# Carrying weight and result place in each row of a routed expert layer, and scattering the results instead of fetching them by index

## The reference

```
logits = xf @ Wg                                  # xf: layernormed tokens, N x 128
topw, topi = top_k(logits, 2); topw = softmax(topw)
comb[n, topi[n]] += topw[n]
gu = einsum('nd,edh->enh', xf, Wgu) + bgu         # 8 experts, 2 x 256 hidden
g, u = split(gu); h = silu(g) * u
eo = einsum('enh,ehd->end', h, Wd) + bd
out = h_in + einsum('end,ne->nd', eo, comb)       # weighted sum of the two experts
```

## Time and profile before

| | |
|---|---|
| median of 3 runs | 820.52 us (817.84 to 821.28) |
| the profiled execution's own time | 824.18 us |
| its span, first to last instruction | 822.4 us |
| busy: PE, DVE, ACT, POOL | 603.9, 430.1, 264.7, 498.1 us |
| mean granted TensorE clock | 0.835 of full |
| indirect DMAs on POOL | 180 to `xbuf`, 180 from `ybuf` |
| chain that ended last | PE 37%, POOL 21%, DVE 14%, issue 13%, DMA 7% |

### The profile page before, as it was taken

The page is one execution under the profiler, slowest core; times in us unless marked ns, Lnnn a source line. Parts: engine busy times, 40 slices in busy tenths (PEclk is TensorE's granted clock), DMA queues, the critical chain, the costliest instruction groups (busy, mean ns, idle before and its releaser), DMA issues.

```text
span 822.4 us, 12791 instructions
## 1 busy us (share of the span) xinstructions
PE 603.9 (73%) x3335; PEld 519.1 (63%) x3335; DVE 430.1 (52%) x1708; ACT 264.7 (32%) x690; POOL 498.1 (61%) x520
## 2 busy tenths in 40 slices
PE   3787645327778788698989986999898969999000
PEld 2687634316567576586878875888787758888000
DVE  4789655343556657265655766355544623445122
ACT  2502122112234432244442543254253324444000
POOL 5602327763655756377677776477777767760674
PEclk9998855557789988698997997899999979999555
DMA  7185000126345533565655663667577768984221
GB/s 152 53 290 148 1 0 26 33 90 186 101 127 153 145 104 106 164 194 150 185 169 154 205 198 106 191 202 218 179 214 235 236 197 257 279 279 147 80 77 61
DMA packets 84597, 125.23 MB, mean 152 GB/s; under 512 B 15044, under 2 KB 57792, under 8 KB 84526
## 3 DMA queue, kind: packets, MB, share of 16 engines
q1 hardware_dynamic: 72526, 101.66, 40.9%
q0 software_dynamic: 11520, 22.35, 9.5%
q10 hardware_dynamic: 480, 0.41, 0.4%
HBM read 84.25 MB, written 43.25 MB: 155 GB/s over the span
## 4 chain that ended last, share of the span: by engine, by line
PE 37%; POOL 21%; DVE 14%; issue 13%; DMA 7%; ACT 3%; SPq 3%; POOLq 0%; DVEq 0%; ACTq 0%
PE gu L587 15%; PE dn L587 11%; POOL gat L1048 8%; POOL xbuf L1034 8%; PE mx L587 5%; POOL rs L966 3%; DMA gat<-ybuf,ypos 3%; PE xTp L765 3%; DMA space<-xbuf 2%; DMA space<-in_x_dram 2%; PE tr L587 2%; ACT x L894 1%; PE tr L719 1%; DVE gat L1485 1%; DVE rec L1268 1%
## 5 line engine op out<-in xcount | busy, mean ns | idle before, releaser
L1034 POOL DMA_INDIRECT xbuf<-x,pos x180 | 186.4, 1035 | 112.9 <-DVE pos L1369 56.0
L587 PE MATMUL gu<-space,wts 128*128 128x256 f32 x912 | 246.0, 410 | 9.1 <-DVE space L1476 9.1
L1476 DVE SCALAR_TENSOR_TENSOR space<-gu,wts,space 128x256 f32<-128x256 f32 x228 | 109.1, 482 | 235.7 <-ACT space L912 173.3
L1048 POOL DMA_INDIRECT gat<-ybuf,ypos x180 | 177.7, 987 | 87.9 <-issue 55.5
L912 ACT ACTIVATE space<-gu,wts 128x256 f32<-128x256 f32 x228 | 109.1, 479 | 305.7 <-PE gu L587 305.3
L587 PEld LDWEIGHTS gu<-space,wts 128*128 128x128 f32 x912 | 174.8, 206 | 32.0 <-DVE space L1476 10.9
L587 PEld LDWEIGHTS dn<-wts,space 128*128 128x128 f32 x912 | 127.9, 204 | 14.1 <-DVE space L1476 7.1
L587 PE MATMUL dn<-wts,space 128*128 128x128 f32 x912 | 129.1, 288 | 5.8 <-DVE space L1476 5.8
L765 PE MATMUL xTp<-cst,space 128*128 128x128 f32 x228 | 51.8, 311 | 40.2 <-DMA space<-xbuf 38.1
L765 PEld LDWEIGHTS xTp<-cst,space 128*128 128x128 f32 x228 | 26.7, 154 | 52.6 <-DMA space<-xbuf 40.8
L966 POOL TENSOR_TENSOR rs<-ve,nhalf 128x4 f32<-128x4 f32 (+2 forms) x39 | 40.4, 1036 | 29.7 <-DVE ve L1281 15.2
(11 more groups left out here) (198 smaller groups left out, 837.8 us busy)
## 6 DMA issues: line engine op xcount, KB each, us to landing
wts<-wall SPq DMA_DIRECT2D x114, 386.0 KB
space<-xbuf SPq DMA_DIRECT2D x114, 128.0 KB, 2.6
ybuf<-space SPq DMA_DIRECT2D x114, 128.0 KB
xbuf<-zero_rows SPq DMA_DIRECT2D x4, 1024.0 KB, 10.5
xt<-in_txt_dram SPq DMA_DIRECT2D x16, 256.0 KB, 3.0
xbuf<-zero_rows SPq DMA_DIRECT2D x32, 128.0 KB
out_dram<-gat SPq DMA_DIRECT2D x16, 256.0 KB
xbuf<-x,pos POOLq DMA_INDIRECT x180
```

Of the source, the lines that this page charges most:

```text
L587: return nc.tensor.matmul(o, l, r, start=a, stop=z_)
L1034: nc.gpsimd.indirect_dma_start(out=xbuf, out_offset=bass.IndirectOffsetOnAxis(pos[0:p, c:c + 1], 0), in_=x2[n % NX2][0:p, m // 2 * D:(m // ...
L1048: nc.gpsimd.indirect_dma_start(out=gat[b][0:p, (k * W4 + j) * D:(k * W4 + j + 1) * D], out_offset=None, in_=ybuf[g], in_offset=bass.Indire ...
L1476: V.scalar_tensor_tensor(hid[q % 4], gu_ps[q % 3][:, SLOT:2 * SLOT], wts[k % NW][:, W_B + HT + t:W_B + HT + t + 1], sil[q % 3], ALU.add, A ...
```

## The change

Rows of `xbuf` become 130 numbers wide: 128 of data, the token's weight for this expert, and the integer place in a new buffer `results` at which the result row belongs. `x2` holds each row twice (one for each expert), the second a copy by ACT. `weights` writes weight and place into them. `row_keep` multiplies the result by the weight that came with the row (two operations in place of one copy), and POOL scatters each tile's 256 result rows with two indirect DMAs to `results` (`scatter_rows`, 228 in all), where a chunk's rows lie in the order of its tokens. SP loads them plainly, one DMA a chunk (`load_results`), and `combine` is two additions. `ybuf`, `store_tile`, `gather`, `places_of_results` and `w2` are gone. Padding rows have places of their own: POOL numbers the zero rows once for the spare regions, waits until these have been written, and numbers them again for `pad`. `text_y` moves from POOL to DVE. The row tile is now held until its results are scattered (`load_tile` waits for tile k-7; 7 buffers in place of 5).

```
@@ slots, buffers
-ITERS = 30
+ITERS = 33
-          z_T=(3, 11), text_decay=(3, 12), text_sums=(3, 13), text_y=(2, 0),
+          z_T=(3, 11), text_decay=(3, 12), text_sums=(3, 13), text_y=(3, 14),
+          ... x_copy=(2, 15),
-NX = 5
+NX = 7
-NG = 4
+NG = 3
+LOADS_AT = by_slot([p for g, (a, b) in enumerate(GROUPS) for p in spread(list(range(a, b)), LOAD_FROM[g], LOAD_TO[g])])
+ROW = D + 2
-    xbuf = nc.dram_tensor("xbuf", (ROW0[-1], D), F32, kind="Internal").ap()
+    xbuf = nc.dram_tensor("xbuf", (ROW0[-1], ROW), F32, kind="Internal").ap()
+    results = nc.dram_tensor("results", (RESULT_ROWS, D), F32, kind="Internal").ap()
@@ SP
-            sp.wait_ge(W.zero_ok, 1)
+            sp.wait_ge(W.spare_ok, 1)
             for g in range(len(GROUPS)):
...
             def load_tile(k):
...
-                wait(sp, W.xTt_ok, k - NX + 1)
+                if k >= NX:
+                    sp.wait_ge(yrow_out[(k - NX) % NYB], stored_before(k - NX))
...
-            def store_tile(k):
...
+            def load_results(n):
+                b, g, p = n % NG, group_of(n), parts(n)
+                if n == GROUPS[g][0]:
+                    for m in range(TILE0[g + 1] - NYB, TILE0[g + 1]):
+                        sp.wait_ge(yrow_out[m % NYB], stored_before(m))
+                wait(sp, W.sum_ok, n - NG + 1)
+                r0 = n * A_CHUNK
+                sp.dma_start(res[b][0:p, 0:2 * width(n) * D].rearrange("p (j c) -> p j c", j=width(n)),
+                             results[r0:r0 + p * 2 * W4, :].rearrange("(p j k) d -> p j (k d)", p=p, k=2)[:, 0:width(n)]
+                             ).then_inc(res_in[b], 16)
@@ ACT
+            def x_copy(n):
+                p, w = parts(n), width(n)
+                act.wait_ge(W.x2_ok, n + 1)
+                rows = x2[n % NX2][0:p, :].rearrange("p (k j c) -> p k j c", k=2, j=W4)
+                copy(rows[:, 1, 0:w, 0:D], rows[:, 0, 0:w, 0:D]).then_inc(W.copy_ok, 1)
@@ row_keep
-                copy(yrow[k % NYB], dn_ps[k % 2][:, 0:SUB * D]).then_inc(W.y_row_ok, 1)
+                for s in range(SUB):
+                    last = nc.scalar.activation(yrow[k % NYB][:, s * D:(s + 1) * D], dn_ps[k % 2][:, s * D:(s + 1) * D], ACT.Copy,
+                                                scale=xrow[k % NX][:, s * ROW + D:s * ROW + D + 1])
+                last.then_inc(W.y_row_ok, 1)
@@ POOL
-            def text_y(n):
...
             def scatter(n, m):
...
-                    pool.wait_ge(W.x2_ok, n + 1)
+                    pool.wait_ge(W.meta_ok, n + 1)
+                    pool.wait_ge(W.w1_ok, n + 1)
+                if m == 1:
+                    pool.wait_ge(W.copy_ok, n + 1)
...
-            def gather(n, j, k):
...
+            def scatter_rows(k):
+                pool.wait_ge(W.y_row_ok, k + 1)
+                for s in range(SUB):
+                    place = xrow[k % NX][:, s * ROW + D + 1:s * ROW + D + 2].bitcast(I32)
+                    nc.gpsimd.indirect_dma_start(out=results, out_offset=bass.IndirectOffsetOnAxis(place, 0),
+                                                 in_=yrow[k % NYB][:, s * D:(s + 1) * D], in_offset=None
+                                                 ).then_inc(yrow_out[k % NYB], 16)
+            def number_pads(base):
+                ids = zero_rows[:, :].bitcast(I32).rearrange("p (e s c) -> p e s c", e=E, s=SUB)[:, :, :, D + 1]
+                return nc.gpsimd.iota(ids, [[SLOT, E], [1, SUB]], base=base, channel_multiplier=SUB)
+            pool.wait_ge(W.zero_ok, 1)
+            pool.wait_ge(W.seen_zero, 2)
+            number_pads(SPARE_ROW).then_inc(W.spare_ok, 1)
+            pool.wait_ge(W.spare, 16 * len(GROUPS))
+            number_pads(PAD_ROW).then_inc(W.pads_ok, 1)
...
-                    for n, j, k in gathers(i, s):
-                        gather(n, j, k)
+                    for k, t in units(i, s):
+                        if t == 1:
+                            if k >= 2 and not any(first_of_group(m) for m in range(k - 1, k + 1)):
+                                scatter_rows(k - 2)
+                            if last_of_group(k):
+                                scatter_rows(k - 1)
+                                scatter_rows(k)
@@ DVE
             def weights(n):
...
-                w0, w1 = [w2[0:p, (n * 2 + k) * W4:(n * 2 + k) * W4 + w] for k in range(2)]
+                meta = x2[n % NX2][0:p, :].rearrange("p (k j c) -> p k j c", k=2, j=W4)
+                wait(dve, W.w1_ok, n)
+                w0, w1 = [meta[:, k, 0:w, D] for k in range(2)]
+                dve.wait_ge(W.x2_ok, n + 1)
+                V.tensor_scalar(meta[:, :, 0:w, D + 1].bitcast(I32), place0[0:p, :].rearrange("p (k j) -> p k j", k=2)[:, :, 0:w],
+                                n * A_CHUNK, None, ALU.add).then_inc(W.meta_ok, 1)
...
-            def places_of_results(g):
...
             def combine(n):
...
+                V.tensor_tensor(rows[:, :, 0], rows[:, :, 0], rows[:, :, 1], ALU.add).then_inc(W.half_ok, 1)
                 dve.wait_ge(W.half_ok, n + 1)
...
+                V.tensor_tensor(h, h, rows[:, :, 0], ALU.add).then_inc(W.sum_ok, 1)
```

More of the change, by code:

```diff
@@ L183, in opens, with loads @@
     return OPENS_AT.get(i * SLOTS + s, [])
-def gathers(i, s):
-    return GATHERS_AT.get(i * SLOTS + s, [])
+def loads(i, s):
+    return LOADS_AT.get(i * SLOTS + s, [])
 def combines(i, s):
@@ L279, in program @@
         top[0] = 6 * ROWS
-        xrow = [part(SUB * D) for _ in range(NX)]
+        xrow = [part(SUB * ROW) for _ in range(NX)]
         xT = [part(SLOT) for _ in range(2)]
@@ L287, in program @@
         h_txt = [part(W4 * D) for _ in range(B)]
[L289 to L292, removed]
+        res_all = sb("res", [P, NG * 2 * W4 * D])
+        res = [res_all[:, i * 2 * W4 * D:(i + 1) * 2 * W4 * D] for i in range(NG)]
+        rows2_raw = res_all[0:2, 0:W4 * D + E * D]
+        rows2_hi = res_all[0:2, W4 * D + E * D:2 * (W4 * D + E * D)].bitcast(F32R)
         wts = [sb(f"wts{i}", [P, W_COLS]) for i in range(NW)]
@@ L303, in program @@
         yT = sb("yT", [P, W4 * D])
-        x2 = [sb(f"x2{i}", [P, W4 * D]) for i in range(NX2)]
+        x2 = [sb(f"x2{i}", [P, 2 * W4 * ROW]) for i in range(NX2)]
         x2T = sb("x2T", [P, W4 * D])
@@ L387, in program @@
         yrow_out = [sem(f"s_yrow_out{i}") for i in range(NYB)]
-        gat_in = [sem(f"s_gat_in{i}") for i in range(NG)]
-        gat_out = [sem(f"s_gat_out{i}") for i in range(NG)]
+        res_in = [sem(f"s_res_in{i}") for i in range(NG)]
         sent = [sem(f"s_sent{i}") for i in range(NX2)]
@@ L425, in stored_before, with loaded_before @@
         def stored_before(k):
-            return 16 * (k // NYB + 1)
-        def gathered_before(n):
-            return 16 * sum(2 * width(m) for m in range(n % NG, n + 1, NG))
-        def out_before(n):
-            return 16 * sum(width(m) if m < IMG_CHUNKS else 1 for m in range(n % NG, n + 1, NG))
+            return 16 * SUB * (k // NYB + 1)
+        def loaded_before(n):
+            return 16 * (n // NG + 1)
         @block.sync
@@ L564, in _ @@
                                 load_tile(k + AHEAD)
-                        else:
-                            if k >= 2 and not any(first_of_group(m) for m in range(k - 1, k + 1)):
-                                store_tile(k - 2)
-                            if last_of_group(k):
-                                store_tile(k - 1)
-                                store_tile(k)
                     if due("text_load", i, s):
@@ L577, in _ @@
                         store_out(n)
+                    for n in loads(i, s):
+                        load_results(n)
                     for g in opens(i, s):
@@ L580, in _ @@
                             load_tile(TILE0[g] + k)
-            for m in range(CHUNKS - NG, CHUNKS):
-                sp.wait_ge(gat_out[m % NG], out_before(m))
+            sp.wait_ge(W.out, 16 * sum(1 if n >= IMG_CHUNKS else width(n) for n in range(CHUNKS)))
         @block.tensor
@@ L764, in tile_T @@
                 for s in range(SUB):
[L765 removed]
+                    last = nc.tensor.transpose(xT_ps[:, s * P:(s + 1) * P], xrow[k % NX][:, s * ROW:s * ROW + D], ident)
                 last.then_inc(W.xTt_ok, 1)
@@ L1502, in _ @@
                             tile_table(g)
-                        if s == RESULT_SLOT and i == GROUPS[g][1] - 1:
-                            places_of_results(g)
                     if due("text_stats", i, s):
```

139 lines of the change are left out of this document (45 added, 94 removed).

## The result

The changed kernel takes **848.67 us** (median of 4 runs, 844.37 to 853.57), the kernel before 820.9 (817.84 to 824.05) beside it: ratio 1.034, 95% interval 1.027 to 1.041. The forecast was 853, and slower. Its profiled span is 851.5 us against 822.4, a growth of 29.1; the forecast had +33.

A forecast was written before the change was run, and what follows sets the result against it. POOL, in-order, was taken to set the pace in stretches 1 and 2, with PE close behind. -38 + 15 + 26 + 13 + 1 + 16 - 3 + 3 = +33 us on 820.5 gave about 853, range 840 to 868.

The forecast's parts named there:

- Tail: After the last `dn`: 40 gathers give way to four scatters and three chunk loads; -38 us (bounds -41, -33).
- Steady state: Stretches 0, 1, 2 (x scatters of tile groups 0 to 2): result scatters replace gathers on POOL; +15, +26, +13 us.
- the floors of stretches 1 and 2: Least growth there, POOL's new demand less the present length: +23.3 and +8.7 us.
- Front: Before chunk 0's `rs`: POOL waits until the numbered spare rows have landed; +16 us (bounds 12, 19), nothing gives it back.
- Behind it POOL has the same work: Behind the front's wait POOL's work is as before, so nothing gives back the +16 us.
- Switches of group: Group starts: the row-tile store gone from SP, -3 us (bounds -8, 0); x scatter's wait for weights, +3, elsewhere hidden.
- Others: `load_tile`'s new wait, the x copy, and stores and sums on engines with room: 0 us; bounds together -3, +5.
- stretch 3: Tiles of group 3: 54 scatters hidden beside full PE, +1 us for the fuller ScalarE (bounds -1, +5).
- `yT` on DVE: `yT` and the new sums on DVE stretch no POOL DMA: 0 us; some +16 if each stretched a scatter.
- B: Rival: in stages 0 to 2 POOL also waits for result rows, +19 to +38 us, about 880; chance 0.17.
- C: Rival, faster: PE sets the pace and POOL's new work fits in, 798 us; chance 0.06.
- D: Rival: the front wait is off the path or lands in a few us, 837 us; chance 0.09.

The follow-up runs named there:

- e7: e3 with a 128x6 power operation of 1.35 us on POOL in place of each of the 228 result scatters; 848.63 us, ratio 1.032.
- e2: The changed kernel with only the first of each tile's two result scatters, half of the result rows left out; 791.66 us, ratio 0.962.
- e3: The changed kernel with no result scatter: SP stores the tiles plainly, the placing of results is left out; 792.36 us, ratio 0.964.
- e5: The kernel before the change with only `text_y` moved from POOL to DVE; 815.56 us, ratio 0.992.
- e1: The changed kernel with POOL numbering the spare regions' zero rows early, ahead of its image work; 834.53 us, ratio 1.0125.
- e12: The changed kernel with a fixed weight of 0.5, so that the x scatter waits for no computed weight; 838.52 us, ratio 1.023 to before.
- e4: The changed kernel with `text_y` back on POOL; 860.61 us, ratio 1.049 to the kernel before.
- e6: e3 with a 128x4 power operation of 1.0 us on POOL in place of each of the 228 result scatters; 820.69 us, ratio 1.001.

## Why the prediction was right

**What bounds the kernel.** Right for the changed kernel: POOL's queue sets the stretches, although busy for only 77%. e7 shows it by replacement, e2 and e3 by taking the load away, until POOL waits 19 and 45 us in stretch 1 at 792. For the kernel before it isn't shown, and e5 speaks against it in stretch 1: six products less on POOL became 6.8 us more of waits and 1.3 us less of length. What else held that stretch, with TensorE busy for 92%, stays open. The forecast only needed the new demand on POOL, 183 us there, to be above TensorE's 147 as well.

**Tail, -38.** Measured -38.9. The last `dn` to the end takes 22.3 us; the last scatter starts at 832.93, 3.8 behind `dn` (3.4 forecast); the first load lands for DVE at 838.73, the last sum starts at 848.33. It ends 19.9 us behind `dn`, 1.5 later than forecast, and from there to the end it takes 2.5 us and not 4.5: two small misses that cancel.

**Steady state, +15, +26, +13: right in kind, and the step that failed in size.** Measured +15.7, +20.0, +5.5; the floors of stretches 1 and 2, +23.3 and +8.7, were missed from below. The added demand was right to 1.7 us. Two inputs were not. POOL's present room was put at 3 and 4 us, and was 6.6 and 6.8: `rs`, `ex` and `yT` were priced from their own start to the next DMA's, with the 0.30 us in which no DMA could have started anyway. For `ex` the DMA ahead of it is this one (POOL's timeline of the kernel before):

```profile
573.87 1.06 POOL L1048 DMA_INDIRECT gat<-ybuf,ypos  x1 [0.30 <-issue]
```

The one behind it starts at 576.24, 2.37 later, so `ex` costs 2.37 - 1.30 = 1.07 and not 1.28. And that the present waits stay is wrong for a resource that grows longer: it gave up 4.7 and 6.8 us of them. Only for stretch 0 did the forecast let waits shrink, from 26 to 6; they went from 33 to 12.

**Front, +16.** Measured +15.1 by the trace; e1 gives back 14.1. "Nothing gives it back" holds, to within the spread of the runs.

**Behind it POOL has the same work.** The work yes, the order of waits no. *Switches of group* had the weights' wait at +1 for each group, "elsewhere POOL is late and it is hidden". In the ramp POOL is not late because of DMAs: the scatter stands right behind the `ex` that its weights are made from, so being late on POOL makes the weights late as well. In the stretches two result scatters can stand between the two (485.93 to 489.77 above) and cover the wait. Ramp +6.3, and the gaps +2.1 and +1.9, of which the -3 for the stores that left SP can't be seen; e12 gives the wait about 10 us in all. This is the term that was put at nothing outside the switches, and it offset most of the excess of the steady state (6.0 and 7.5 us). That the sum, +33 against +29, is closer than its parts is luck: without the offset it would have been some 14 us too high.

***Others*, stretch 3, `yT` on DVE.** 0 and +1 forecast; +0.2 measured behind stretch 2 (in e1, e4 and e7 this piece is about 3 us shorter than in the profiled execution of the changed kernel, so it is known no better than that). For `yT` the traces show that the product stretches no scatter.

**Rivals.** B, 880: no wait of over 0.6 us in the stretches names ScalarE's rows, and e7. (Behind stretch 2 POOL waits for them at nearly every tile, some 1.1 us each, beside a TensorE that is busy for 96% from 744 to 829 us.) C, 798: a scatter would have had to cost less than 1.09 us in place of 1.30; e6 comes nearest to that case, 0.97 a piece (with nothing written) and 820.69, no change. So the breaking point is nearer 0.97. D: e1 rules it out.

## What to carry to other kernels

Measure how full an in-order engine is by its waits, not by its busy share, and price an instruction by how much later it makes the next one that was going to run anyway. When you add work to the engine that sets the pace, the waits that it still has are what gives way first. Where a value that an engine computes comes back to it through another engine, the distance between the two places in its program is what counts: a late engine doesn't hide such a wait, if nothing else stands between the two.

## What the runs showed of the hardware that I had not expected

- The 0.30 us behind an indirect DMA on POOL holds only the next indirect DMA (0.96 busy, 1.26 from start to start). A power operation behind it starts after 0.02 us.
- Fetch or scatter, rows of 512 or of 520 bytes, makes no difference to POOL: 0.95 to 0.96 us in each kind where nothing else disturbs it.
- Between such DMAs a power operation of 128x4 keeps POOL for 1.0 us and one of 128x6 for 1.35, more than the DMA's busy time itself.
- An indirect DMA on POOL that starts while DVE's scan of 128x512 runs ends some 0.8 us after the scan does (0.75 to 0.85 in 26 cases in the changed kernel and e4), so it takes up to 1.98 us instead of 0.96. A DVE product of 128x512 (0.69 us) does not do this.
